# The first half of x is issued by ScalarE ahead of its two small loads, instead of third by SyncE

## What is computed

```
x = x + tanh(g_xattn[0]) * attention_0(layernorm(x), ctx)      # scores from ctx alone, 128 wide
x = x + tanh(g_ffn[0])   * ffn_0(layernorm(x))                 # rms norm, int8-like activations, ternary weights
x = x + tanh(g_xattn[1]) * attention_1(layernorm(x), ctx)      # 16 heads of 128, rms norm on q and k
x = x + tanh(g_ffn[1])   * ffn_1(layernorm(x))                 # 64 experts, 8 chosen, one shared
```

```
query = ctx @ Wq.T + bq;  key = ctx @ Wk.T + bk
attention = softmax(query @ key.T);  x_m = layernorm(x).T mixed by attention
```

## Time and profile before

| | us |
|---|---|
| median of 3 runs (622.93 to 625.71) | 623.46 |
| the profiled execution's own time | 623.48 |
| its span in the trace | 621.7 |

### The profile page before, as it was taken

How to read it: one execution, slowest core, us unless ns; L and a number is a source line. 1 busy time by engine, 2 the same in 40 slices (tenths; PEclk the granted TensorE clock), 3 DMA queues, 4 the chain that set the end, 5 groups by cost and what they waited for, 6 DMA issues and landing times.

```text
span 621.7 us, 11583 instructions
## 1 busy us (share of the span) xinstructions
PE 604.4 (97%) x3634; PEld 522.1 (84%) x3634; DVE 474.9 (76%) x1133; ACT 423.1 (68%) x1080; POOL 232.9 (37%) x280
## 2 busy tenths in 40 slices
PE   8789989999999999999999999999999999999997
PEld 6556879999999999999998888888887888887886
DVE  4999887777777688778775787778877777777775
ACT  5998979888888888789897435364544444443442
POOL 6699797766666566566653020000000000000000
PEclk9999999999999999999999999999999999999999
DMA  8332220100000000000030454453856466555630
GB/s 298 141 102 71 65 71 26 53 1 2 2 2 2 2 2 2 1 2 1 3 116 13 128 169 144 131 157 103 215 166 168 117 173 166 164 155 148 195 127 34
DMA packets 33653, 56.47 MB, mean 91 GB/s; under 512 B 12800, under 2 KB 13504, under 8 KB 33600
## 3 DMA queue, kind: packets, MB, share of 16 engines
q1 hardware_dynamic: 33312, 55.82, 29.9%
q10 hardware_dynamic: 288, 0.00, 0.0%
HBM read 53.45 MB, written 1.31 MB: 88 GB/s over the span
## 4 chain that ended last, share of the span: by engine, by line
PE 85%; DVE 6%; POOL 5%; issue 2%; ACT 1%; DMA 1%; DVEq 0%; SPq 0%; ACTq 0%
PE bank L289 25%; PE bank L291 24%; PE bank L290 24%; PE bank L867 4%; PE bank L842 2%; PE bank L834 2%; POOL w L528 1%; POOL u L516 1%; DMA wqk<-in_qk 1%; DVE attT_lo L1860 1%; DVE stats L1680 1%; PE bank L714 0%; DVE rowmax L1848 0%; DVE hs L1774 0%; POOL rk L534 0%
## 5 line engine op out<-in xcount | busy, mean ns | idle before, releaser
L1395 ACT ACTIVATE inter_hi<-inter 128x512 fp32r<-128x512 f32 x63 | 39.8, 632 | 140.5 <-DVE inter L1959 140.5
L289 PE MATMUL bank<-xnT_hi,front_hi 128*128 128x512 f32 (+1 forms) x260 | 102.0, 392 | 0.0
L291 PE MATMUL bank<-xnT_hi,front_lo 128*128 128x512 f32 (+1 forms) x260 | 101.7, 391 | 0.0
L290 PE MATMUL bank<-xnT_lo,front_hi 128*128 128x512 f32 (+1 forms) x260 | 101.7, 391 | 0.0
L1963 DVE TENSOR_TENSOR inter_lo<-inter,inter_hi 128x512 fp32r<-128x512 f32 x63 | 43.6, 692 | 37.5 <-ACT inter_hi L1395 37.0
L1352 ACT ACTIVATE att<-bank,shift,rq 128x256 f32<-128x256 f32 x128 | 71.3, 571 | 0.0
L1848 DVE TENSOR_REDUCE rowmax<-bank 128x2 f32<-128x512 f32 x64 | 43.7, 686 | 27.4 <-PE bank L291 27.3
L550 POOL TENSOR_TENSOR att<-att,rowinv 128x512 f32<-128x512 f32 x60 | 62.0, 1053 | 5.2 <-DVE rowinv L1865 5.2
L534 POOL TENSOR_TENSOR rk<-msq,minus_half 128x4 f32<-128x4 f32 x32 | 32.9, 1027 | 78.9 <-DVE msq L1837 78.9
L1932 DVE TENSOR_TENSOR prod<-gate_s,bank 128x512 f32<-128x512 f32 x63 | 43.3, 687 | 21.9 <-PE bank L291 19.8
L290 PEld LDWEIGHTS bank<-xnT_lo,front_hi 128*128 128x128 f32 x260 | 48.9, 188 | 11.3
(11 more groups left out here) (266 smaller groups left out, 1802.0 us busy)
## 6 DMA issues: line engine op xcount, KB each, us to landing
w_all<-w_rows SPq DMA_DIRECT2D x128, 128.0 KB, 2.9
raw<-in_expert_w SPq DMA_DIRECT2D x32, 384.0 KB, 3.6
wvo_raw<-in_expert_w SPq DMA_DIRECT2D x16, 384.0 KB, 3.5
e_more<-in_expert_w SPq DMA_DIRECT2D x16, 384.0 KB, 3.6
raw<-in_head_qk SPq DMA_DIRECT2D x8, 384.0 KB, 3.4
wvo_raw<-in_head_vo SPq DMA_DIRECT2D x4, 384.0 KB, 3.1
w_keep<-in_head_vo SPq DMA_DIRECT2D x4, 384.0 KB, 3.0
gate_raw<-in_gate_wT SPq DMA_DIRECT2D x2, 704.0 KB, 8.8
```

What stands on the lines that cost most here:

```text
L289: pe.matmul(out, l_hi, r_hi_, start=start, stop=False, skip_group_check=True)
L290: pe.matmul(out, l_hi, r_lo_, start=False, stop=False, skip_group_check=True)
L291: return pe.matmul(out, l_lo, r_hi_, start=False, stop=stop, skip_group_check=True)
L1395: act.activation(inter_hi[:, slot, :], inter[:, slot, :], ACT.Copy).then_inc(a_Ihi, 1)
```

## The change

The issue of x half 0 leaves SP's list, where it was third, and becomes the first instruction of ACT's list, ahead of bqk and gains. Half 1 stays in SP's list and is now third. The semaphores and all waits are the same.

```diff
         def _(sp):
             sp.dma_start(ctxT_raw[:, :], ctxT).then_inc(l_ctxT, 16)
             sp.dma_start(wqk0[:, :, :], qk0).then_inc(l_qk0, 16)
-            for h in range(2):
-                sp.dma_start(x[:, 4 * h:4 * h + 4, :], x_tok[:, 4 * h:4 * h + 4, :]).then_inc(l_x[h], 16)
+            sp.dma_start(x[:, 4:8, :], x_tok[:, 4:8, :]).then_inc(l_x[1], 16)
...
             def load_table(function):
                 act.activation(spare[:, :], tg[:, 0:1], function)
 
+            act.dma_start(x[:, 0:4, :], x_tok[:, 0:4, :]).then_inc(l_x[0], 16)
             act.dma_start(bqk[:, :], bias0).then_inc(l_small, 16)
             act.dma_start(gains_raw[:, :], gains).then_inc(l_small, 16)
             high_ctxT()
```

## The result

The changed kernel takes 628.58 us (median of 13 runs, 625.95 to 629.29), the kernel before in the same measurement 623.46 (13 runs, 622.86 to 627.18). The ratio is 1.0053, with a 95% interval of 1.0036 to 1.0070: about 3.3 us slower. The interval leaves no change out; the size is just over the 0.5% that the prediction had taken for what can be told. The two medians lie further apart (5.1 us), and what is over the 3.3 is chance: the runs of both kernels fall into groups some 2.5 us apart, the upper group has 6 of the 13 runs of the kernel before (625.07 and over) and 7 of the 13 of the changed one (628.58 and over), and one run more or less decides in which group the median falls. The lowest runs, 622.86 and 625.95, are 3.1 apart.

A forecast was written before the change was run, and what follows sets the result against it. PE bounds most of the kernel, and the change can only shift the start of its chain, which begins with wqk's landing. 623.48 + 1.80 for wqk's delay, all other terms 0, gives 625.3 us; range for 8 in 10: 623.0 to 626.9.

The forecast's parts named there:

- x half 0 has nothing to give: At the start, x half 0 has 0.50 us and 0.38 us to spare; bringing it earlier alone gains nothing.
- The issues cost nothing: SP's list loses an issue, worth 0; ACT's extra issue of 0.41 to 0.45 us hides in its idle 1.83, cost 0.
- The half of x beside ctxT and wqk: At the first loads, alternating queues delay wqk by 1.80 us, bounds 0 to 2.74; first query_key starts at 7.04.
- bqk and gains hidden by 0.33 us: Before the first copy_qk: gains lands at 8.13, copy_qk is due at 8.46 because of PE; cost 0.
- the prediction's own sign: At the first copy_qk: release by PE was expected; waiting for bqk or gains would prove the prediction wrong.
- rival 2: At the first copy_qk: small loads bqk and gains become the gate, +3.0 us at worst, 626.5; chance 0.12.
- The clock does not fall: At the first query_key: PE's granted clock was expected to stay up despite 2.1 us of idle after the warming matmuls.
- Rival 3: At PE's start: clock falls to 1.2 GHz, 4.16 us more, with the 1.80 together 5.96, so 629.4; chance 0.03.
- A start later by some time ends everything later by the same: Whole chain: lists are fixed, so a shift of the first query_key moves everything behind it by the same time.
- the forecast's own mechanism: At the first loads: wqk's delay from queues sharing, bounds 1.22 to 2.74 us, so 624.7 to 626.2; the forecast keeps 0.68.
- slower by over 0.5%: Whole kernel: needs 626.6 us, by rival 3, part of rival 2, or the forecast's upper end with an unlucky median; 0.11 together.

The follow-up runs named there:

- e1: Changed kernel with ACT issuing bqk and gains ahead of x half 0; ratio to before 1.0016, lowest run 623.38 us.
- e5: Changed kernel with a semaphore of its own for gains, so the first copy_qk waits for bqk alone; ratio to before 1.0053, lowest run 626.46 us.
- e9: Changed kernel with a separate semaphore for gains and 16 warming matmuls in place of 8; ratio to before 1.0046, lowest run 625.22 us.
- e11: Changed kernel once more, unaltered, for a second profile; ratio to before 1.0051, five runs, 626.40 to 628.01 us.
- e3: Changed kernel with 16 warming matmuls in place of 8; ratio to before 1.0060, lowest run 626.07 us.
- e4: Kernel before with bqk and gains moved to SP's queue behind both halves of x; ratio to before 1.0098, lowest run 627.47 us.
- e6: Changed kernel with both halves of x on ACT's queue, ahead of bqk and gains; ratio to before 1.0090, lowest run 628.98 us.
- e10: Kernel before with 16 warming matmuls and nothing else; ratio to before 1.0023, lowest run 624.64 us.
- e2: Changed kernel with bqk and gains on SP's queue right behind wqk; ratio to before 1.0074, lowest run 626.27 us.
- e7: Kernel before with 9 warming matmuls in place of 8; ratio to before 1.0003, lowest run 623.03 us.
- e8: Kernel before with wqk first in SP's list and ctxT as two transfers with a semaphore each; ratio to before 1.0004, lowest run 623.35 us.

## Why the prediction was right, and where not

**x half 0 has nothing to give.** Right. Its data came 1.25 sooner and DVE's idle time only moved behind the statistics: 5.16 us in front of the maxima.

**The issues cost nothing.** Right for ACT: it still idled 3.0 us before high_ctxT.

**The half of x beside ctxT and wqk.** Right, and near in size: I took 1.80 and the start was 2.04 late, in the second profile 2.15. The strict turns that the Trainium skill describes (DMA: Bandwidth & Descriptors, on queues, rings and completion order) would have given up to 2.74; e1 shows that turns are what happens, since 3 KB in small packets hold back 512 KB. The bound was not reached, since the 1152 KB had all landed at 7.16 and not at 7.85: the two queues together moved them faster than the one had. Why is not shown. The 1.80 came from a rate and not from the turns, so that it is so near owes something to luck.

The Trainium skill says on the same page (on issuing engines not being separate DMA queues) that issuing from several engines only saves the sequencer's time. The runs contradict the "only": the choice of the queue changed who waits for whom, by 2.1 us for wqk and 3.9 us for gains from issue to landing.

**bqk and gains hidden by 0.33 us.** Wrong, and by the prediction's own sign: the first copy_qk was to be released by PE. This is the step that failed: I had gains landing 1.22 behind wqk, by the rate of the stretch 7.9:9.15. It landed at 9.66 (1.66 + 8.0), 2.5 behind wqk's 7.16 (1.18 + 6.0), and released the first copy_qk. I had it run beside half 1 of x, and this was the error: half 1 landed at 8.54 (1.64 + 6.9), and gains 1.12 after it. The small packets were not as quick as one for one with the large ones (107 to 144 in 7:8.5), and the last of them ran beside the gate weights (13 of q10 against 128 of q1 in 8.5:10). Why they fell behind is not shown. The threshold that the prediction gave, 1.55 behind wqk, was crossed, so that rival 2 is what the profile shows, with +3.12 at copy_qk where that rival had +3.0.

**The clock does not fall.** Wrong too: PE had the low clock in its first pairs. Rival 3 had a chance of 0.03, against which I held a stretch at 18:20 in which an idle PE kept its clock. In both profiles of the changed kernel the three pairs ran slowly, 4.47 and 4.51 for 3.10, and in the second, as in e5, the record shows the clock at half there. Its price was 1.4 (4.47 - 3.10), not the 4.16 that I had worked out from a doubling: before's own first matmuls had been slow already, which I had not seen (below). Most of it lay under the wait for gains: without it the first copy_qk would have been released by PE at about the same moment (e5: 9.66). It added 0.29 in the end (maxima 3.41 late, copy_qk 3.12). So of the 3.41, 2.04 are wqk's delay, and the other 1.37 are the gate and the slow pairs, either of which was enough for nearly all of it.

**A start later by some time ends everything later by the same.** Right to 0.4: 3.41 at the maxima and at the first residual; in the second profile 3.37 at both and 3.0 at the end.

**The numbers.** The point, 625.3, was 1.8 over before; measured is a factor of 1.0053, 3.3 us. The forecast's size was therefore a little over half of the effect; the missing part is the gate with the slow pairs under it. 623.46 times 1.0053 is 626.8, just inside the upper end of 626.9, and that end had been drawn for rival 2 and not for the forecast's own mechanism, which ended at 626.2. The median of the runs, 628.58, lies above the range, since by one run it fell into the upper group. That the ratio is inside by 0.1 is luck. To "slower by over 0.5%" I had given 0.11. The measured ratio is just over that line, with an interval on both sides of it. That chance was too small, because rivals 2 and 3 were each taken as alone, and both came.

## What to carry to other kernels

A transfer that goes out on a second queue doesn't come in addition. In this kernel it took turns with the first one, about packet for packet, so whatever small thing stood behind it or beside it paid with a whole large packet per turn. Before moving a load to the idle queue, write down for both queues which packets will stand side by side, and follow the smallest loads too, since 2 KB on a shared semaphore can gate more than the 512 KB that one was thinking of. And when two delays end at about the same moment at one instruction, taking away either one shows next to nothing; take away both before you call either harmless.

## What was not expected of the hardware

**The clock's record begins late.** In the first profiles of both kernels the column of the granted clock stands at 1.00 from the start. The pairs of query_key say otherwise. Instructions of this line in the kernel before and in the changed kernel, ns min/median/max:

```profile
L714 PE MATMUL bank<-ctxT_raw,wqk x8: 592/592/951, 5.2 to 10.5; 128*128 128x512 f32 x8
L713 PE MATMUL bank<-ctxT_raw,wqk x6: 592/989/1190, 7.3 to 11.2; 128*128 128x512 f32 x6
```

and in e9, with PE kept busy up to its start:

```profile
L714 PE MATMUL bank<-ctxT_raw,wqk x6: 592/592/667, 7.7 to 9.9; 128*128 128x512 f32 x6
```

The median of 989 for 592 is what the lower level of 1.2 GHz looks like: in e11, where the column says 0.58 for 7.28:10.60, the same matmuls have a median of 1004. So the column can't be read before the first change that was recorded, and "full throughout" doesn't hold for the first microseconds of the kernel before, where one matmul took 951. Durations of equal matmuls can be read.

**The groups of runs.** Times differ by about 2 to 2.5 us from execution to execution of the same kernel. In the profiled executions two things go with it: when PE's clock rises at the start, and whether it falls again at about 23 to 26, in a stretch in which PE has gaps. The profile of e1 (625.44, pairs of 4.95 in all) is a run of its upper group, and the two profiles of the changed kernel (628.91 and 626.50) differ in the fall at 24. The fall was there in the first profile of the changed kernel, e3, e4, e5, e6, e9 and e10 (granted clock 0.51 to 0.82 in 24.2:31.2), and not in before, e1, e2, e7, e8 and e11 (1.00). Where it was there, the span had 1.8 to 2.0 more over before's than the first residual had (after, e9, e10). What decides it in one execution stays open. More warming didn't prevent it: it was there in all three profiles with 16 warming matmuls. Only one execution of each run was profiled, so that the same two things make the groups in the other runs is likely and not shown.
